# Trial scores on quarters of the array, two units at the end of every second step

## What is computed

```python
x = _L0_conv_ref(x, ...)                  # neighbourhood attention, window 7x7, 4 heads; MLP 64-256-64
t = _to_tokens(x)                         # (2, 1024, 64)
t = t + _L1_attn_ref(_ln_t(t), ...)       # full attention over 1,024 tokens, 8 heads of 64
t = t + _L1_ffn_ref(_ln_t(t), ...)        # 33 steps, most of them masked off by the routing
```

```python
q = (x @ Wq).reshape(b, t, h, e) * scale
k = (x @ Wk).reshape(b, t, h, e) * scale
dot = jnp.einsum('bqhe,bkhe->bhqk', q, k)
att = jax.nn.softmax(dot, axis=-1)
out = jnp.einsum('bhqk,bkhe->bqhe', att, v).reshape(b, t, h * e)
```

## Time and profile before

| | us |
|---|---|
| median of 3 runs (614.12 to 620.15) | 614.19 |
| the profiled execution | 615.03 |
| its span | 613.2 |
| PE busy | 548.1 (89%) |
| DVE busy | 405.8 (66%) |
| ACT busy | 316.9 (52%) |
| POOL busy | 51.1 (8%) |
| L1557, reductions of the trials on DVE, 128 | 156.3 |
| L766, score products on PE, 1,024 | 135.6 |
| L789, value products on PE, 512 | 132.8 |
| L750, trial products on PE, 512 | 81.0 |

### The profile page before, as it was taken

The page is one execution under the profiler, slowest core; times in us unless marked ns, Lnnn a source line. Parts: engine busy times, 40 slices in busy tenths (PEclk is TensorE's granted clock), DMA queues, the critical chain, the costliest instruction groups (busy, mean ns, idle before and its releaser), DMA issues.

```text
span 613.2 us, 11018 instructions
## 1 busy us (share of the span) xinstructions
PE 548.1 (89%) x4271; PEld 296.8 (48%) x4272; DVE 405.8 (66%) x740; ACT 316.9 (52%) x584; POOL 51.1 (8%) x106
## 2 busy tenths in 40 slices
PE   6999998999699989999999999999999933799962
PEld 5554654555244435454555554445555410266621
DVE  5555547455886745886877677776663357798763
ACT  2645445834155574556655556556566433465440
POOL 6030233212110000000000010000000000000000
PEclk9999999977889999999999999999999958899977
DMA  5000000000000000000000000000000000000001
GB/s 114 1 2 1 2 3 1 1 1 2 1 1 1 1 1 2 2 0 1 2 1 0 2 2 1 1 10 1 1 1 0 1 4 6 10 1 1 2 0 34
DMA packets 9514, 3.33 MB, mean 5 GB/s; under 512 B 8820, under 2 KB 9079, under 8 KB 9463
## 3 DMA queue, kind: packets, MB, share of 16 engines
q1 hardware_dynamic: 8182, 2.61, 1.9%
q10 hardware_dynamic: 1281, 0.01, 0.1%
HBM read 2.09 MB, written 0.52 MB: 4 GB/s over the span
## 4 chain that ended last, share of the span: by engine, by line
PE 78%; DVE 9%; issue 7%; ACT 3%; POOL 1%; POOLq 0%; DVEq 0%; ACTq 0%
PE PS L766 18%; PE PS L789 17%; PE PS L750 8%; PE PS L671 4%; PE PS L685 4%; PE PS L698 3%; PE PS L522 2%; PE PS L712 2%; PE PS L730 2%; PE PS L494 2%; PE PS L506 2%; PE PS L805 2%; PE PS L994 2%; PE PS L568 2%; PE PS L586 1%
## 5 line engine op out<-in xcount | busy, mean ns | idle before, releaser
L1557 DVE TENSOR_REDUCE most<-PS 128x2 f32<-128x1024 f32 x128 | 156.3, 1223 | 71.9 <-PE PS L750 71.2
L1193 ACT ACTIVATE PT<-PS 128x512 f32<-128x512 f32 x256 | 138.8, 596 | 75.6 <-PE PS L766 75.2
L766 PE MATMUL PS<-qS,aS 128*64 128x512 f16 x1024 | 135.6, 383 | 2.0 <-ACT PT L1193 1.9
L789 PE MATMUL PS<-PT,V 128*64 128x512 f32 x512 | 132.8, 592 | 0.0
L766 PEld LDWEIGHTS PS<-qS,aS 128*64 128x64 f16 x1024 | 61.3, 111 | 62.1 <-issue 20.4
L750 PE MATMUL PS<-aS,qS 128*64 128x512 f16 x512 | 81.0, 391 | 4.4 <-DVE most L1557 4.0
L1149 ACT ACTIVATE prob<-sbias,negm 128x320 f32<-128x320 f32 (+1 forms) x64 | 34.3, 538 | 42.9 <-DVE negm L1603 42.6
L789 PEld LDWEIGHTS PS<-PT,V 128*64 128x64 f32 x512 | 40.0, 137 | 19.5 <-issue 0.8
L750 PEld LDWEIGHTS PS<-aS,qS 128*64 128x64 f16 x512 | 32.1, 111 | 30.3 <-DVE most L1557 8.4
L671 PE MATMUL PS<-ident 128*128 128x256 f16 x128 | 39.9, 312 | 6.3 <-DVE negm L1603 5.4
L1312 POOL TENSOR_TENSOR rstd<-var,minus_half 128x8 f32<-128x8 f32 (+1 forms) x9 | 13.5, 1504 | 355.4 <-DVE var L1420 355.4
(11 more groups left out here) (192 smaller groups left out, 670.4 us busy)
## 6 DMA issues: line engine op xcount, KB each, us to landing
xall<-in_x_dram SPq DMA_DIRECT2D x2, 256.0 KB, 4.4
out_dram<-x SPq DMA_DIRECT2D x4, 128.0 KB, 2.1
w<-in_L_attn_Wq_dram SPq DMA_DIRECT2D x2, 128.0 KB, 2.5
w<-in_L_attn_Wk_dram SPq DMA_DIRECT2D x2, 128.0 KB, 2.7
w<-in_L_attn_Wv_dram SPq DMA_DIRECT2D x2, 128.0 KB, 2.7
fc<-in_L_conv_fc_w_dram SPq DMA_DIRECT2D x2, 64.0 KB, 2.4
wu<-in_L_attn_Wu_dram SPq DMA_DIRECT2D x2, 64.0 KB, 2.4
w1s<-in_L_ffn_ffn_w_dram SPq DMA_DIRECT2D x2, 64.0 KB, 2.1
```

The costliest lines, as they stand in the source:

```text
L766: mm = pe.matmul(PS[h0:h0 + C, lane, :], aS[:, k0 + h0:k0 + h0 + C], qS[:, part, lane, toks], start=(part == 0), stop=(part == 1))
L789: mm = pe.matmul(PS[cols, 6 + g % 2, :], V[:, img * NT + kt, cols], PT[:, g % 2, lane, kt, :], start=(kt == 0), stop=(kt == NT - 1))
L1193: act.activation(PT[:, g % 2, lane, phase, :], PS[:, lane, :], ACT.Exp).then_inc(c1["exped"], 1)
L1557: dve.tensor_reduce(most[:, g % 2, u // 2, u % 2, :], banks, AX.X, ALU.max, negate=True)\
```

## The change

Trial scores are computed from the high halves alone: 64 rows of queries against 64 rows of keys. Lane 0 takes rows 0 to 63 of the array with `aS[0:64]`, lane 1 rows 64 to 127 with `aX`, a second copy of the high half of the input, kept in the upper half of `kS` (free at that time) and made by one more ACT copy for each of four blocks. So the four products of a unit lie on four different quarters of the array. PE does no trial at an even step; at the end of an odd step it does two units, t+11 and t+12. DVE reduces the first of them at its old place in the odd step, the second at the start of the even step.

```diff
--- before.py
+++ after.py
@@ -223,6 +223,7 @@
         hS = aS
+        aX = kS[C:P, 0, :]
         Z = PTrow[:, 0:2 * B * TOK].rearrange("p (h t) -> p h t", h=2)
@@ -745,10 +746,11 @@
                 q0 = toks.start + qt * P
                 k0 = img * TOK + half * BLK
-                for lane in range(2):
-                    for h0 in (0, C):
-                        mm = pe.matmul(PS[h0:h0 + C, try_bank(a) + lane, :], qS[:, 0, lane, q0 + h0:q0 + h0 + C],
-                                       aS[:, k0:k0 + BLK], start=True, stop=True)
+                for h0 in (0, C):
+                    for lane, keys in enumerate((aS[0:C], aX)):
+                        mm = pe.matmul(PS[h0:h0 + C, try_bank(a) + lane, :],
+                                       qS[C * lane:C * lane + C, 0, lane, q0 + h0:q0 + h0 + C],
+                                       keys[:, k0:k0 + BLK], start=True, stop=True)
                 mm.then_inc(c1["tried"], 1)
@@ -894,8 +896,6 @@
                 if 0 <= t < UNITS:
                     scores(t)
-                if 0 <= t + AHEAD < UNITS:
-                    try_scores(t + AHEAD)
                 if 0 <= t - LAG_VAL < UNITS:
                     glob_values(t - LAG_VAL)
@@ -911,6 +911,9 @@
                     turn_shift(g + 1)
+                if t % 2 and t + AHEAD < UNITS:
+                    try_scores(t + AHEAD)
+                    try_scores(t + AHEAD + 1)
 
                 if t in (TURN_T, HIDDEN_T[1], MLP_T, INPUT_T):
@@ -1094,6 +1097,7 @@
                     act.wait_ge(side_filled, order[key] + 1)
+                    act.activation(aX[:, toks], side_bank(key)[C:P, :], ACT.Copy)
                     act.activation(aS[:, toks], side_bank(key), ACT.Copy).then_inc(side_high, 1)
@@ -1755,6 +1759,8 @@
             for t in STEPS:
                 g, phase = divmod(t, NT)
+                if t % 2 == 0 and t + AHEAD < UNITS:
+                    greatest(t + AHEAD)
                 if 1 <= g <= NG and phase in (Y_PHASE + 1, Y_PHASE + 2):
                     weigh_outputs(g - 1, phase - Y_PHASE - 1)
```

## The result

The changed kernel takes **658.20 us** (median of 4 runs, 649.53 to 658.64), the kernel before 617.17 us (4 runs, 614.12 to 620.77): 1.0653 times as long, interval [1.0588, 1.0718]. The profiled execution took 658.27 us, its span is 656.5 us; before, 615.03 and 613.2.

The account below looks back on a forecast made before the run. PE was taken as the bound, busy 50.00 of 50 us in mid full attention. Terms summing to +29.3 on the profiled 615.03 gave 644.3, a median of 643.5, predicted as 644 us; range 630 to 665.

Parts of the forecast that it names:

- two waits of PE for DVE's list: Each full group: PE waits 1.15 us before `project` in phase 4 and 2.00 before `turn_shift` in phase 6.
- The rival in which they never come: DVE is ready when PE reaches `project` and `turn_shift`, leaving only the pairs' saving: 601 us, chance 0.04.
- the first rival: Trial products: the four quarters do not all run together, a unit stays 0.43 us: 665 us, chance 0.13.
- What a pair saves: Trial pair on PE: 0.43 us streaming plus 0.20 for changing the array, in place of 0.86, saving 0.23.
- 12 groups at +2.23: Groups 1 to 12: both waits less four pair savings of 0.23 cost 2.23 us a group, +26.8.
- group 2: Phases 2 and 3: gelu holds ACT, DVE catches up; phase 4's wait and that pair's saving fall away: -0.9 us.
- other DVE and ACT work, groups 1 to 12: Side work between reductions or ahead of a needed operation adds to waits: +3.4 us of the +4.0 forecast.
- group 0 with its side work: Group 0 has no outputs to weigh or add, +0.3 us; with the divisions of t = 5, +0.9.
- groups 13 and 14: Group 13 has pairs and no pieces, -0.9 us; group 14 has two pairs, -0.5.
- the start: Two more copies for image 0 and three pairs while DVE's reductions bound PE: +0.5 us, bounds 0 and 2.
- The rival had a chance of 0.10: Waits idle PE in phases 4 to 6, so its clock falls: 655 us, or far above 665 if every group.
- my own case: The kernel takes 636 to 654 us, slower by the waits less the pairs' saving; chance 0.62.

Follow-up runs that it names:

- e4: The change with the wide products of the kernel before in place of quarters, still in pairs and in the change's order, without the copies: 658.54 us, ratio 1.0678.
- e2: The change with DVE's second reduction back at its old place and `add_outputs` one step later, behind `low_query`: 612.31 us, ratio 0.9951.
- e10: e8 with pairs of wide products (128 rows by 64 columns), no quarters and no copies: 615.12 us, ratio 0.9989.
- e9: The change with DVE's second reduction at its old place in phase 4 alone: 638.35 us, ratio 1.0391.
- e1: The change with DVE's second reduction of each pair back at its old place in the even step: 620.97 us, ratio 1.0111.
- e3: The change without pairs: quarters and copies kept, one unit a step between scores and values, DVE in the old order: 624.46 us, ratio 1.0107.
- e6: e2 with the copies made by DVE from SBUF in place of ACT from PSUM: 610.19 us, ratio 0.9964.
- e8: e6 with DVE's side work (key tables, moments of image 1, divisions) moved to steps where nothing waits behind it: 611.46 us, ratio 0.9962.
- e5: The kernel before with the four extra ACT copies of the high half alone, read by nobody: 617.80 us, ratio 1.0103.

## Why the prediction was right, and where it was 14 us short

**The mechanism is shown.** The forecast rested on two waits of PE for DVE's list, 1.15 and 2.00 us. Read from the rows they are 1.2 and 2.0; taken away one after another they are worth 1.13 and 1.92, 3.05 in all where 3.15 was forecast. They come without quarters (e4) and go with the quarters in place (e2). The rival in which they never come falls with the wait before L731.

**The quarters run together**, as taken from L638: the foursomes are 0.24 apart, not 0.43, so the first rival is out. The Trainium skill (TensorE: Matmul & The Clock Gate, Part 3, measured speedup) gives 3.07 times for four row strips. By that I had estimated 0.28 a foursome; the trace's 0.24 on 64 by 64 quarters lies between that and the ideal 0.215.

**What a pair saves was taken too large.** Forecast 0.43 + 0.20; measured in group 7: 0.12 ahead of the pair (`project` ends at 358.57 + 0.43, the pair starts 0.12 later), 0.48 for two foursomes, 0.08 to the scores and 0.02 by which the values behind them are late, so 0.70. The streaming is 0.05 dearer than the rate of side-by-side strips, the change of the array 0.02. A pair saves 0.14 to 0.16 (rows; e2 and e10), not 0.23.

**The sum, term by term** (forecast 644.3 for the profiled execution, measured 658.27):

| term | forecast | measured |
|---|---|---|
| 12 groups at +2.23 | +26.8 | 12 x 2.48 = +29.8 |
| group 2 | -0.9 | -1.1 |
| other DVE and ACT work, groups 1 to 12 | +3.4 | +3.8 |
| group 0 with its side work | +0.9 | +1.3 |
| groups 13 and 14 | -1.4 | -1.6 |
| a lower clock inside the stage | 0 | about +4.8 |
| the start | +0.5 | +5.3 |
| after the stage | 0 | +1.1 |

(The forecast's +4.0 for side work is split here: the divisions of t = 5, 0.6, stand with group 0.) Three terms make 12.6 of the 14 us; the rest is small.

- *The clean group*, 0.25 too low each: 0.35 because a pair saves less, less 0.10 for the shorter waits. The step that was mis-sized is the change of the array and the streaming of a pair, 0.63 forecast and 0.70 measured.
- *The clock inside the stage.* The rival had a chance of 0.10 and came in part: not long stretches, but three of 3.4 us each, at 268.9, 316.7 and 408.8 us. The windows of the change show the last two (PE, PEld, DVE, ACT, POOL busy, then PEclk):

```profile
316.00:321.00 5.00, 4.31 (x30) 1.77 (x32) 1.11 (x3) 2.26 (x4) 0.00 (x0) 0.66 0.00 0
408.00:413.00 5.00, 5.00 (x37) 1.83 (x33) 1.55 (x2) 2.63 (x5) 0.00 (x0) 0.66 0.00 0
```

  A granted clock of 0.66 over 5 us is 3.4 us at 0.50, the lower level of 1.2 GHz. What PE did just before these two (its timeline; the brackets are the waits):

```profile
316.69 0.64 PE L821 MATMUL PS<-ident,shift 128*64 128x128 f16 x8 [2.22 <-issue]
...
407.76 0.41 PE L821 MATMUL PS<-ident,shift 128*64 128x128 f16 x8 [2.44 <-issue]
```

  Each of the three began within 1.1 us of the end of a wait of 2.2 to 2.5 us, in the groups where side work lengthens the wait of phase 6; after the 1.84 of a clean group the clock never fell. In five traces with the long waits (the change twice, e4, e9, and the change with DVE's copies) there are 19 waits of 2.1 to 2.5 us, 10 of them followed by such a stretch; in e1, e2, e3, e6, e8 and e10 there are no such waits between 244 and 475 us, and no such stretch between 190 and 470. The price is read from the same group with and without one: group 3 of the change takes 23.91, of the run with DVE's copies 22.40; group 9 24.75 and 23.15: 1.5 to 1.6 us each, and by e9 about as much in group 5. Why one long wait is followed by it and another isn't, stays open.
- *The start.* About 1.3 us of the 5.3 are the copies (e5, e1 against e10). I had bounded the start by 2 and taken 0.5; what I left out is that DVE's softmax work for PE, and through it PE, is late by the chain behind the copies. The rest goes with the clock of the first layer, which differs from run to run: ahead of the first scores 29.9 us of the change's trace ran at the lower clock, 23.8 of the trace before, and 14.0 of the change's second trace. Its first scores come at 175.89 in the one trace and 170.45 in the other, and between 166.1 and 185.2 over all kernels here. With the second trace's start the forecast would have missed by 8.5.

The median, 658, lies above the 636 to 654 that I had given my own case, with 0.62; it is inside the range only because that was kept open to 665 for the rivals. The run of the change once more has a median of 654.01. So the experiments bear out the account of the groups, while the clock and the start came out dearer than I took them; that the median still lies in the range says nothing for those two terms.

Where the stretches at the lower clock in the first layer fall, and so whether a run takes 605 or 614 us (e8), is not settled by these runs.

## What to carry to other kernels

Two productions put together put their two consumers together in the list of an engine that takes its work in order; whatever else waits behind them is late by one consumer's time, and that is the price to count before the saving. So after batching, walk down that engine's list, and put the short operation that the bottleneck waits for ahead of the long one that nobody needs soon. Here the two waits cost 3.05 us in each full group, and the same products with the consumers put right lose nothing (e2, ratio 0.9951).

## What was not expected of the hardware

- Four f16 products of 512 columns on the four 64 by 64 quarters start within 0.01 us and hold PE 0.24 us, two of which share each half of the columns; going from 64-column strips to quarters costs about 0.12 and back about 0.10.
- Stretches of 3.4 us at a granted clock of 0.50 that begin within 1.1 us of the end of waits of PE of 2.1 to 2.5 us (10 of 19 such waits), in a stage that is at 1.00 from its first few us on.
- A copy of 64x512 f16 within SBUF takes DVE 0.29 us; ACT's copy of the same shape out of PSUM 0.59.
- A wait of PE that a DVE operation ends can be booked as "issue": 1.84 before L821, where DVE's L1553 ended 0.10 us earlier.
